# A two-layer feature-interaction kernel: the whole fp32 group moved from fifth to fourth place, its half-filled tile beside layer 0's last tile

## The reference, cut to what matters

```
z0   = einsum('bid,bjd->bdij', e, e)            # 39*39 products
cur0 = relu(z0 @ W0)                            # 128 channels: 64 next_h, 64 direct0
z1   = einsum('bid,bjd->bdij', e, next_h)       # 39*64 products
cur1 = relu(z1 @ W1)                            # 128 channels
z    = sum over d of concat([direct0, cur1])    # 192 features
h    = relu(concat([z, dense]) @ W_top1 + b_top1)
h    = relu(h @ W_top2 + b_top2);  y = h @ W_top3
```

## Time and profile before

| | |
|---|---|
| median of 3 runs | 449.19 us |
| profiled execution: time | 449.96 us |
| profiled execution: span | 448.1 us |
| mean granted TensorE clock | 0.97 |
| PE busy | 405.8 us (91%) |
| DVE busy | 347.6 us (78%) |
| ACT busy | 227.2 us (51%) |
| POOL busy | 270.8 us (60%) |

### The profile page before, as it was taken

How to read it: one execution, slowest core, us unless ns; L and a number is a source line. 1 busy time by engine, 2 the same in 40 slices (tenths; PEclk the granted TensorE clock), 3 DMA queues, 4 the chain that set the end, 5 groups by cost and what they waited for, 6 DMA issues and landing times.

```text
span 448.1 us, 4257 instructions
## 1 busy us (share of the span) xinstructions
PE 405.8 (91%) x1446; PEld 238.8 (53%) x1446; DVE 347.6 (78%) x197; ACT 227.2 (51%) x224; POOL 270.8 (60%) x180
## 2 busy tenths in 40 slices
PE   0263299999999999999999999999999999999997
PEld 0221056565656565656565565656565656565744
DVE  0301676998989898989898989899898989998900
ACT  2122346556464646465564655655646464645413
POOL 5777888888888888888888888888810000000000
PEclk9958589999999999999999999999999999999999
DMA  8369269493959495868668596959493949752000
GB/s 286 97 152 182 43 145 186 108 213 84 216 117 216 100 205 107 198 136 196 133 155 171 138 193 143 188 125 208 98 211 84 218 96 212 165 129 59 1 0 0
DMA packets 25740, 64.03 MB, mean 143 GB/s; under 512 B 8512, under 2 KB 16661, under 8 KB 19446
## 3 DMA queue, kind: packets, MB, share of 16 engines
q1 hardware_dynamic: 19128, 60.55, 60.4%
q0 software_dynamic: 5632, 1.35, 3.2%
q10 hardware_dynamic: 958, 1.86, 1.2%
HBM read 59.87 MB, written 3.84 MB: 142 GB/s over the span
## 4 chain that ended last, share of the span: by engine, by line
PE 87%; issue 8%; SPq 4%; DMA 0%; ACT 0%
PE acc L495 22%; PE acc L525 14%; PE acc L517 13%; PE acc L518 13%; PE acc L533 12%; PE sums L485 5%; PE spread L506 3%; PE spread L562 2%; SPq L243 1%; SPq L232 1%; SPq L195 1%; SPq L221 0%; PE sums L551 0%; PE sums L553 0%; SPq L205 0%
## 5 line engine op out<-in xcount | busy, mean ns | idle before, releaser
L282 POOL DMA_INDIRECT found<-in_table_dram,rows_sb x176 | 270.6, 1538 | 56.6 <-issue 53.0
L423 DVE TENSOR_TENSOR z_lo<-z,z_hi 128x2048 fp32r<-128x2048 f32 x64 | 146.2, 2285 | 2.3 <-ACT z_hi L325 1.3
L325 ACT ACTIVATE z_hi<-z 128x2048 fp32r<-128x2048 f32 x64 | 122.3, 1911 | 16.8 <-DVE z L415 15.0
L415 DVE TENSOR_TENSOR z<-x_wide,h 128x2048 f32<-128x2048 f32 x48 | 109.8, 2288 | 12.5 <-ACT h L309 8.7
L495 PE MATMUL acc<-squares,w 128*128 128x512 f32 x224 | 114.7, 631 | 0.0
L517 PE MATMUL acc<-z_hi,w_hi 128*128 128x512 f32 x256 | 106.9, 417 | 0.7 <-ACT cur L318 0.7
L518 PE MATMUL acc<-z_hi,w_lo 128*128 128x512 f32 x256 | 100.3, 392 | 0.0
L301 ACT ACTIVATE squares<-sums 128x1024 f32<-128x1024 f32 x64 | 58.8, 919 | 78.7 <-PE sums L485 70.7
L525 PE MATMUL acc<-z_lo,w_hi 128*128 128x512 f32 x256 | 90.5, 475 | 0.0
L415 DVE TENSOR_TENSOR z<-spread,h 128x2048 f32<-128x2048 f32 x32 | 73.1, 2283 | 1.3 <-PE spread L506 1.2
L525 PEld LDWEIGHTS acc<-z_lo,w_hi 128*128 128x128 f32 x256 | 47.0, 188 | 32.3 <-issue 26.8
(11 more groups left out here) (41 smaller groups left out, 111.2 us busy)
## 6 DMA issues: line engine op xcount, KB each, us to landing
x_wide<-x_rows SPq DMA_DIRECT2D x96, 512.0 KB
x_parts<-x_rows SPq DMA_DIRECT2D x62, 64.0 KB
found<-in_table_dram,rows_sb POOLq DMA_INDIRECT x176
w_sb<-in_w_dram SPq DMA_DIRECT2D x1, 1280.0 KB, 7.2
x_rows<-found_hi SPq DMA_DIRECT2D x32, 26.8 KB
x_rows<-found SPq DMA_DIRECT2D x32, 26.8 KB
x_rows<-found_lo SPq DMA_DIRECT2D x30, 26.8 KB
z<-in_select_dram ACTq DMA_DIRECT2D x1, 576.0 KB, 7.9
```

The lines of the kernel that those rows point to most:

```text
L282: pool.indirect_dma_start(out=found[:, b, s * D:s * D + D], out_offset=None, in_=table, in_offset=bass.IndirectOffsetOnAxis(ap=rows_sb[:, ...
L325: nc.scalar.activation(z_hi[:, n % RING], z[:, n % RING], ACT.Copy).then_inc(hi_done, 1)
L415: nc.vector.tensor_tensor(z[:, n % RING], x, h[:, c % 2, :].unsqueeze(1).to_broadcast([P, QUADS, N]), ALU.mult).then_inc(multiplied, 1)
L423: nc.vector.tensor_tensor(z_lo[:, n % RING], z[:, n % RING], z_hi[:, n % RING], ALU.subtract).then_inc(lo_done, 1)
```

## The change

Four edits go together.

1. `WHOLE = 3`: group 3 (the fourth) is the one in plain fp32; groups 0, 1, 2 and 4 are split. `SPREAD` and `WIDE` change from [1, 3] and [0, 2, 4] to [1, 4] and [0, 2, 3]. The left-over half tile is now the upper half of the whole group's first tile (its weights there are zero).
2. Layer 0's last tile has its 49 pairs in partitions 64 to 112 instead of 0 to 48; `square` handles only these 64.
3. `contract0` of that tile goes away for chunks 1 to 15. In its place `contract1_whole` interleaves the two half-filled tiles, 256 columns at a time: lower 64 rows into `acc1`, upper 64 rows into `acc0`. The remaining three tiles follow with all 512 columns.
4. ACT does `high_part(n+1)` ahead of `evict0(c+1)`. PE's last `contract1_lo` of a chunk comes in the next chunk's first step, and for the last chunk after the loop.

```diff
-SPREAD = [1, 3]
-WIDE = [0, 2, 4]
-SPREAD_FROM = [0, 24, 12, 36]
-WIDE_FROM = [[4, 8], [16, 20], [28, 32]]
+SPREAD = [1, 4]
+WIDE = [0, 2, 3]
+SPREAD_FROM = [0, 24, 12, 35]
+WIDE_FROM = [[4, 8], [16, 20], [28, 31]]
+WHOLE = 3
 def is_v(n):
-    return n % G < VG
+    return n % G != WHOLE
...
+                rows = slice(0, P) if n == 2 else slice(HALF, P)
...
-                nc.scalar.activation(squares[:, q % RING0, 0:n, :], sums[:, 0:n, :], ACT.Square).then_inc(squared, 1)
+                nc.scalar.activation(squares[rows, q % RING0, 0:n, :], sums[rows, 0:n, :], ACT.Square).then_inc(squared, 1)
...
+                    if n + 1 < G * CHUNKS and is_v(n + 1):
+                        high_part(n + 1)
                     if c + 1 < CHUNKS and g == ND - 1:
                         evict0(c + 1)
                         if c + 2 < CHUNKS:
                             square(ND * (c + 2))
-                    if n + 1 < G * CHUNKS and is_v(n + 1):
-                        high_part(n + 1)
...
+            def contract0_part(q, cols):
+
+                return nc.tensor.matmul(acc0[:, cols], w0[HALF:P, T0 - 1, :], squares[HALF:P, q % RING0, 0, cols],
+                                        start=False, stop=(cols.stop == N))
...
-            def contract1_whole(n):
+            def contract1_whole(n, beside=None):
                 r = n % RING
                 pe.wait_ge(multiplied, n + 1)
-                for a in range(QUADS):
+                if beside is not None:
+                    pe.wait_ge(squared, beside + 1)
+                for k in range(2):
+                    cols = slice(N // 2 * k, N // 2 * k + N // 2)
+                    nc.tensor.matmul(acc1[:, cols], w1_sb[0:HALF, VT, :], z[0:HALF, r, 0, cols],
+                                     start=False, stop=False)
+                    if beside is not None:
+                        last = contract0_part(beside, cols)
+                if beside is not None:
+                    last.then_inc(contracted0, 1)
+                for a in range(1, QUADS):
                     last = nc.tensor.matmul(acc1[:, :], w1_sb[:, VT + a, :], z[:, r, a, :],
-                                            start=False, stop=(a == QUADS - 1))
+                                            start=False, stop=False)
                 last.then_inc(contracted1, 1)
...
-                        contract0(ND * (c + 1) + g)
+                        if g != WHOLE:
+                            contract0(ND * (c + 1) + g)
...
-                        contract1_whole(n)
-
+                        contract1_whole(n, ND * (c + 1) + ND - 1 if c + 1 < CHUNKS else None)
+
+            contract1_lo(G * CHUNKS - 1)
```

More of the change, by code:

```diff
@@ L59, in is_v, with slot1 @@
 def is_v(n):
-    return n % G < VG
+    return n % G != WHOLE
 def v_count(n):
-    return n // G * VG + min(n % G + 1, VG)
+    return n // G * VG + n % G + (n % G < WHOLE)
+def slot1(g):
+    return QUADS * (VG if g == WHOLE else g - (g > WHOLE))
 def pairs():
@@ L493, in contract0 @@
                 pe.wait_ge(squared, q + 1)
+                rows = slice(0, P) if d < ND - 1 else slice(HALF, P)
                 for a, t in enumerate(DUOS[d]):
-                    last = nc.tensor.matmul(acc0[:, :], w0[:, t, :], squares[:, q % RING0, a, :],
+                    last = nc.tensor.matmul(acc0[:, :], w0[rows, t, :], squares[rows, q % RING0, a, :],
                                             start=(t == 0), stop=(t == T0 - 1))
                 last.then_inc(contracted0, 1)
+            def contract0_part(q, cols):
+                return nc.tensor.matmul(acc0[:, cols], w0[HALF:P, T0 - 1, :], squares[HALF:P, q % RING0, 0, cols],
+                                        start=False, stop=(cols.stop == N))
             def spread_out(n):
@@ L515, in contract1_hi @@
                 for a in range(QUADS):
-                    t = QUADS * g + a
+                    t = slot1(g) + a
                     nc.tensor.matmul(acc1[:, :], w1_hi[:, t, :], z_hi[:, r, a, :], start=(t == 0), stop=False)
@@ L524, in contract1_lo @@
                 for a in range(QUADS):
-                    last = nc.tensor.matmul(acc1[:, :], w1_hi[:, QUADS * g + a, :], z_lo[:, r, a, :],
-                                            start=False, stop=False)
+                    last = nc.tensor.matmul(acc1[:, :], w1_hi[:, slot1(g) + a, :], z_lo[:, r, a, :],
+                                            start=False, stop=(g == G - 1 and a == QUADS - 1))
                 last.then_inc(contracted1, 1)
-            def contract1_whole(n):
+            def contract1_whole(n, beside=None):
                 r = n % RING
                 pe.wait_ge(multiplied, n + 1)
-                for a in range(QUADS):
+                if beside is not None:
[9 more added lines that the diff above has]
+                for a in range(1, QUADS):
                     last = nc.tensor.matmul(acc1[:, :], w1_sb[:, VT + a, :], z[:, r, a, :],
-                                            start=False, stop=(a == QUADS - 1))
+                                            start=False, stop=False)
                 last.then_inc(contracted1, 1)
@@ L637, in layout @@
     for t, tile_pairs in enumerate(pairs()):
-        for r, (i, j) in enumerate(tile_pairs):
+        for r, (i, j) in enumerate(tile_pairs, HALF if t == T0 - 1 else 0):
             w0a[t * P + r] = from_w0[i, j]
@@ L658, in layout @@
                     select[row:row + 2, T0 + i, HALF * a:HALF * a + HALF] = 1.0
-                    w1[HALF * a:HALF * a + HALF, QUADS * g + q] = from_w1[f]
+                    w1[HALF * a:HALF * a + HALF, slot1(g) + q] = from_w1[f]
     for i, g in enumerate(WIDE):
         for a in range(2):
-            f = WIDE_FROM[i][a]
-            w1[HALF * a:HALF * a + HALF, QUADS * g:QUADS * g + QUADS] = from_w1[f:f + QUADS].transpose(1, 0, 2)
+            for k in range(QUADS):
+                f = WIDE_FROM[i][a] + k
+                if a == 0 or f >= WIDE_FROM[i][0] + QUADS:
+                    w1[HALF * a:HALF * a + HALF, slot1(g) + k] = from_w1[f]
     def by_tile(a):
```

## The result

The change makes the kernel slower. The ratio to the kernel before is 1.0463 [1.0424, 1.0503]; the profiled execution took 472.27 us, span 470.5. Two of its four executions are compared, 472.27 and 468.13; the other two, 544.98 and 605.09, ran at a mean granted TensorE clock of 0.76 and 0.655 and are left out. The same kernel was timed again with the first experiments (e1_again): 468.14 us (467.02 to 469.22), ratio 1.0431 [1.0415, 1.0446], span 465.2, the fastest of its five executions. The prediction said 466.3, between 461 and 476.

A forecast was written before the change was run, and what follows sets the result against it. PE's queue was taken as the bound, DVE close behind. Added: 11.8 over 13 intervals, 1.4 in the last, 1.3 for chunk 1, 2.6 in the tail, together 17.1; forecast 466.3 us, range 461 to 476.

The forecast's parts named there:

- 5 x 0.215 = +1.08: PE's block of two half tiles: eight 256-column records, partly side by side, form a chain of five record times, +1.08 us.
- Rival 1: The half tiles on PE do not run side by side: block 1.72, 475 us; chance 0.18 together with rival 2.
- rival 2: Half tiles side by side, but each load waits for its row group: block 1.61, 474 us; 0.18 together with Rival 1.
- 3 x 0.20 = +0.60: PE's loop: three more changes of row tiling a chunk, at 0.20 us each.
- The boundary ... +0.95: Chunk boundary on PE: the product behind the last `contract1_lo` waits bare for `acc1`'s eviction, +0.95 us at 14 more boundaries.
- PE's 24.56 stands: PE's loop of 24.56 us a chunk, +0.91, sets the period, just above DVE's 24.43.
- rival 3: DVE decides alone, the block at its lower bound 0.86: period 24.43, 464.6 us; inside the likeliest case's 0.68.
- h is now two-fold late ... 5.39 us: DVE's loop: multiply to multiply on `h` takes 5.39 us, 3.19 idle where it was 0.68, making 24.43 a chunk.
- DMA work ... I cost both at nothing: DMA queues: same bytes with more time, third wide transfer issued and wanted one step sooner; cost nothing.
- Chunk 1's `h`, +1.3: Ahead of the steady intervals: chunk 1's `h` comes 1.3 us later, behind `contract1_lo`, a tiling change and the block.
- The last interval, +1.4: Last interval from `h` to `h`: no `add_up` left on PE, 23.03 before becomes DVE's 24.43, +1.40 us.
- the tail, +2.6: After the last `h`: one more `low_part` (2.20) before the top layer and two tiling changes (0.40), +2.6 us.

The follow-up runs named there:

- e6: e4 with gathers for the first three chunks only, so its output is not the reference's: 448.3 us, ratio 0.9986.
- e12: e6 with layer 0's last tile back in its own place and the whole group's four tiles over 128 rows: 454.55 us, ratio 1.012.
- e5: The changed kernel with gathers for the first three chunks only, so its output is not the reference's: 466.89 us, ratio 1.0397.
- e3: The changed kernel with PE doing the fifth group's `contract1_lo` ahead of the next chunk's `add_up` and `contract0`: 468.99 us, ratio 1.0436.
- after: The changed kernel as first profiled, with nothing further changed: 472.27 us in the profiled execution, ratio 1.0463 to the kernel before.
- e4: e3 plus, at the fifth group, DVE's `low_part` ahead of the multiply on `h` and ACT's `split` ahead of `high_part`: 454.98 us, ratio 1.0146.
- e7: e4 with the third wide transfer of a chunk issued one step later: 456.75 us, ratio 1.0169.
- e9: e4 with `SPREAD` [1, 3] and `WIDE` [0, 2, 4] as before the change, the half tile last in its group: 460.41 us, ratio 1.0238.
- e10: The changed kernel with ACT's `evict0` back ahead of `high_part`, as in the kernel before: 488.5 us, ratio 1.0879.
- e2: The changed kernel with layer 0's last tile back in its own place and the whole group's four tiles over 128 rows: 471.1 us, ratio 1.0489.

## Why the prediction was right, point by point

- **"layer 0's last `contract0` ... -1.72", "5 x 0.215 = +1.08".** The tiles do run side by side; the chain of five links was wrong, it is four: 0.86, the lower bound (1.07 from the first start to the next tile, less a change of 0.20). I took matmuls to be started whole and in order; the trace shows record by record. Rival 1 is out, and rival 2 too: the loads at 219.74 and 219.75 start while the matmuls of 219.63 and 219.64 stream in the same rows.
- **"3 x 0.20 = +0.60".** Right as far as the runs tell: with 0.86, three changes and no boundary wait the sum is 23.39, and e6 has 23.43. The pair's worth has the same check: 0.86 less streaming, two changes (0.40) more, is 0.46; e12 against e6 measured 0.48.
- **"The boundary ... +0.95".** The wait is there, 0.69 as PE notes it. On PE's loop it counts as much as was said: e6's 23.43 and 0.95 make 24.38, and e5's trace has 24.41. For the time it counts nothing by itself (e3).
- **"PE's 24.56 stands".** This step failed, by a little: with the pair at 0.86 PE's loop is 24.41, and DVE's decides. That was rival 3 (24.43, 464.6), which the prediction had inside its likeliest case.
- **"h is now two-fold late ... 5.39 us", "21.24 + 3.19 = 24.43".** The mechanism is right, the wait is 3.21; 5.48 start to start, since `evict0` starts 1.94 behind `high_part` (220.51 to 222.45) where I took 1.82. The loop is 24.54. That the block was 0.22 less on one engine and the loop 0.11 more on the other, and the sum stayed where it was, +0.89 a chunk for +0.91, is luck.
- **"The wait for `found_hi` ... should vanish".** In undisturbed chunks it does. In disturbed ones it comes back as a wait of `split` for the gathered rows.
- **"DMA work ... I cost both at nothing".** Wrong: 3.9 us in the profiled execution, 1.8 in e1_again. The pace of GpSimd was the matter, of which the prediction has nothing; it depends on where in DVE's work a gather falls (in after 1.89 us or more beside some operations, 1.5 or less beside others, see below).
- **Chunk 1's `h`, +1.3.** Between -0.7 and +0.75, so this term is not confirmed; this stretch has loads in it, and moves by 1.4 us between executions of one kernel.
- **The last interval, +1.4, and the tail, +2.6.** 1.26 and 2.61 (e1_again): 2.20 up to the first top-layer matmul (15.97 for 13.77) and 0.41 behind it, as worked out. The 1.6 more in the first profile is the clock (0.50 from 438.7 to 442.1).

The sum of 17.1 was met by e1_again's span (465.2 - 448.1 = 17.1), in part by luck: 1.8 of gather waits and 0.5 at the start stand for the missing 2.0 of chunk 1, and it is the fastest of its five executions. In the medians the change costs 18.9 (449.21 to 468.14). The profiled execution of after has 22.4 in span, by more gather waits, the clock, and chunk 1.

## What to carry to other kernels

Where two engines' loops lie as close together as here (24.54 and 24.41 us), work out both to the end and name the one that decides last: here a wait taken from the other brought nothing (e3), and work saved there brought only a part (the pair gives 0.32 a chunk while DVE decides next, 0.48 when PE does). A tile that is put beside another must be weighed with what it makes late: here layer 0 ends later, the multiply that it feeds waits 3.2 us, and a chunk is 0.89 longer in spite of the pair. Even with DVE's loop shortened and the boundary wait and the gathers gone, a chunk is 23.43 for 23.65 (e6): 0.2 is all that the change had to offer. An engine that is "66% busy" can still be late: GpSimd was so in after, where a gather took from 0.99 to 6.74 us, depending on what DVE did when it started. Look at its rows of single instructions.

## What the runs showed of the hardware

- **fp32 matmuls in two row groups.** Each fp32 matmul leaves two records (L558: six for three matmuls); two such matmuls in the lower and upper 64 rows have their records side by side in order, starts within 10 ns, at 256 columns as at 512. Two 64-row tiles cost what one 128-row tile costs, 0.86, plus two changes of tiling of 0.20 (e12 less e6 is 0.48 for 0.86 less 0.40).
- **Gathers and VectorE.** A gather alone takes 1.0 us (in after from 5 to 13 us, where DVE stands still). Which ones take longer shows in after by what DVE does when they start: of 66 that start while DVE works on two operands from SBUF (`z<-x_wide,h`, `z_lo<-z,z_hi`, once `w_lo<-w_sb,w_hi`) each takes 1.89 or more; of 110 that start in a multiply with its factor from PSUM (`z<-spread,h`), in a short operation or while DVE stands still, none takes over 1.5. Before, it is 82 of 83 and none of 93. (In e4, e7, e9 and e10 some that start late in a multiply from PSUM are long too.) Every one in the eleven traces with all gathers that takes over 1.5 (779 of them) ends 0.86 to 0.88 us behind the end of a DVE operation; where the next follows at once, this is 0.95 behind its start: 207.42 + 6.74 = 214.16, with DVE at 213.21; 214.46 + 4.69 = 219.15, with DVE at 218.21.
- **Gathers that miss a boundary.** The gather of 6.74 lets DVE's starts at 208.81 and 211.01 go by, that of 4.69 the one at 216.00. In after, a gather that starts 1.39 us ahead of DVE's next start, from `z_lo` to `z<-x_wide`, misses it, 8 of 8 times; before, none lies so, and none lasts over 2.92. In e2 ten of 4.54 us miss one boundary. Where this happens in after, 11 gathers take 25.84 us (197.52 to 223.36), longer than the chunk's 24.54, with nothing between them but the 0.30 of issue; so GpSimd loses its lead, and `split` waits. Over four chunks it takes 99.9 us (145.85 to 245.76), as do four intervals from `h` to `h`, 3 x 24.53 + 26.31: in that stretch GpSimd is the pace, as its 59% of the chain says. What decides whether a gather catches DVE's gap was not found (e7, e9).
- **The clock.** Behind a PE wait of 2.4 us, and one of 0.69 after it, the granted clock was 0.50 for 3.4 us of the last chunk in after (from 428.5) and in e1_again (from 425.6). A second such stretch came in after, behind a wait of 1.69 us (from 438.7), and not in e1_again, where the wait was 1.42 us and the clock 1.00 behind it (435 to 438).
